# Issuing the values products of a head in one row of nine units, with eighteen probability buffers

## The reference

```
N_HEADS = 6
B, T, C = x.shape                      # 32, 1024, 96
hs = C // H                            # 16
k = (x @ Wk).reshape(B, H, T, hs)      # a plain reshape: 192 "heads" of 1024 rows
q = (x @ Wq).reshape(B, H, T, hs)
v = (x @ Wv).reshape(B, H, T, hs)
wei = einsum('bhtd,bhsd->bhts', q, k) * C ** (-0.5)
wei = where(tril(ones(T, T)), wei, -inf)
wei = softmax(wei, axis=-1)
out = einsum('bhts,bhsd->bhtd', wei, v)
```

## Time and profile before

| | before |
|---|---|
| time, median of 3 runs | 3497.25 us (3497.21 to 3500.66) |
| the profiled execution's own time | 3498.39 us |
| its span | 3496.7 us |
| TensorE busy | 3229.6 us, 92% |
| weight loads busy | 1775.0 us, 51% |
| VectorE busy | 2397.6 us, 69% |
| ScalarE busy | 2069.6 us, 59% |
| GpSimd busy | 766.1 us, 22% |
| granted TensorE clock, mean | 0.968 |

### The profile page before, as it was taken

How to read it: one execution, slowest core, us unless ns; L and a number is a source line. 1 busy time by engine, 2 the same in 40 slices (tenths; PEclk the granted TensorE clock), 3 DMA queues, 4 the chain that set the end, 5 groups by cost and what they waited for, 6 DMA issues and landing times. The chain is left out here.

```text
span 3496.7 us, 85276 instructions
## 1 busy us (share of the span) xinstructions
PE 3229.6 (92%) x28894; PEld 1775.0 (51%) x28894; DVE 2397.6 (69%) x4745; ACT 2069.6 (59%) x3730; POOL 766.1 (22%) x1529
## 2 busy tenths in 40 slices
PE   4999999999985999999999999999999989988896
PEld 2444545445542555555555555555555544443442
DVE  4566566566654777777777777777777755656665
ACT  2677777777753555555555555555555546555554
POOL 0233444444444122121221212212122100000000
PEclk8999999999997999999999999999999989989998
DMA  1122222222224555545455455554555531211221
GB/s 28 37 77 95 94 78 81 94 94 94 95 77 126 99 92 93 97 89 97 93 93 97 89 97 93 93 97 89 97 93 93 97 67 45 82 45 39 78 72 45
DMA packets 889092, 291.02 MB, mean 83 GB/s; under 512 B 840625, under 2 KB 873682, under 8 KB 889042
## 3 DMA queue, kind: packets, MB, share of 16 engines
q1 hardware_dynamic: 889042, 290.37, 37.5%
HBM read 101.55 MB, written 88.08 MB: 54 GB/s over the span
## 5 line engine op out<-in xcount | busy, mean ns | idle before, releaser
L906 ACT ACTIVATE at_probs<-at_ps_keys 128x512 f32<-128x512 f32 x1728 | 992.8, 600 | 738.7 <-PE at_ps_keys L838 616.4
L924 DVE TENSOR_REDUCE at_unit_max<-at_ps_queries 128x1 f32<-128x512 f32 (+3 forms) x2304 | 1153.7, 551 | 196.0 <-PE at_ps_queries L824 164.3
L824 PE MATMUL at_ps_queries<-at_turned 96*128 96x512 bf16 (+3 forms) x2304 | 681.5, 332 | 61.2 <-DMA at_turned<-at_spread 31.1
L838 PE MATMUL at_ps_keys<-at_turned 128*128 128x128 bf16 (+3 forms) x3456 | 660.5, 273 | 2.1 <-ACT at_probs L906 1.4
L857 PE MATMUL at_ps_values<-at_probs,at_v 128*32 128x128 f32 x13824 | 497.1, 277 | 0.1
L857 PEld LDWEIGHTS at_ps_values<-at_probs,at_v 128*32 128x32 f32 x13824 | 342.2, 109 | 134.8 <-ACT at_probs L906 68.6
L784 POOL TENSOR_TENSOR at_v<-at_stacks,at_one 128x128 f32<-128x128 f32 x192 | 77.0, 401 | 1383.6 <-PE at_ps_values L857 1341.7
L838 PEld LDWEIGHTS at_ps_keys<-at_turned 128*128 128x128 bf16 x3456 | 255.5, 97 | 223.9 <-issue 80.2
L824 PEld LDWEIGHTS at_ps_queries<-at_turned 96*128 96x128 bf16 x2304 | 191.7, 97 | 315.1 <-DVE at_unit_max L924 224.9
L827 PE MATMUL at_ps_queries<-mask_queries,ident_bf 128*128 128x128 bf16 x1536 | 330.3, 221 | 0.0
L650 PE MATMUL cb_ps_qkv<-w_attn,cb_x 96*128 96x384 f32 x512 | 198.2, 512 | 5.8 <-ACT cb_a_squares L568 4.3
(11 more groups left out here) (201 smaller groups left out, 4656.4 us busy)
## 6 DMA issues: line engine op xcount, KB each, us to landing
qkv_rows<-cb_packed SPq DMA_DIRECT2D x32, 1536.0 KB, 8.1
at_stacks<-qkv_rows SPq DMA_DIRECT2D x192, 256.0 KB, 3.3
cb_x<-in_x_dram SPq DMA_DIRECT2D x32, 384.0 KB, 3.7
cb_x_again<-in_x_dram SPq DMA_DIRECT2D x32, 384.0 KB, 4.4
x_after_conv<-cb_x SPq DMA_DIRECT2D x32, 384.0 KB, 5.0
attention_rows<-at_att SPq DMA_DIRECT2D x384, 32.0 KB, 2.2
ff_att_rows<-attention_rows SPq DMA_DIRECT2D x32, 384.0 KB, 4.0
ff_x<-x_after_conv SPq DMA_DIRECT2D x32, 384.0 KB, 4.7
```

Of the source, the lines that this page charges most:

```text
L824: mm = pe.matmul(pq[:, u % QBANKS, 0:n], QT[0:STACK, slot, qb * P:(qb + 1) * P], KT[0:STACK, slot, k0:k0 + n], start=True, stop=True)
L838: mm = pe.matmul(pk[:, bank_k, c0:c0 + n * P], KT[:, slot, kb * P:(kb + 1) * P], QT[:, slot, q0 * P:(q0 + n) * P], start=(c0 == 0), stop=True,
L906: act.activation(PR[:, slot_unit % RING, :], pk[:, slot_unit % KBANKS, :], ACT.Exp, scale=scale).then_inc(S["probs"], 1)
L924: dve.tensor_reduce(MX[:, r % 2, qb, k0 // BANK:k0 // BANK + 1], pq[:, u % QBANKS, 0:n], AX.X, ALU.max).then_inc(S["unit_max"], 1)
```

## The change

Two constants of `causal_attention` change:

```diff
     SLOTS = 4
-    RING = 6
-    BATCH_UNITS = 3
+    RING = 18
+    BATCH_UNITS = 9
     QBANKS, KBANKS = 3, 2
     LAG = 4
     VALUES_LAG = LAG + 2
```

## The result

The changed kernel takes 3576.9 us (median of 4 runs, 3574.36 to 3577.99) against 3497.23 us (4 runs): a ratio of 1.0226, 95% interval 1.0208 to 1.0244. It is 80 us slower where 59 was forecast. The profiled execution took 3576.5 us with a span of 3574.8 us, 78.1 us above the span of before.

A forecast was written before the change was run, and what follows sets the result against it. A loop over VectorE (q8 to q4) and TensorE (q7 to q8) bounds the kernel at 8.96 us a head; +1.31 - 0.40 - 0.43 - 0.17, 0.30 with exact quotients, over 190 heads plus 2 us gives 3556 us, range 3530 to 3600.

The forecast's parts named there:

- The long row: At step 5, 48 more values records between q7 and q8 add 1.31 us a head (1.18 to 1.36) to VectorE's wait.
- the rival of the slow long row: The 72 records at step 5 run slower than a short batch: +0.36 us a head, 3624 us; chance 7%.
- a batch of 72 records longer than 2.1 us: Sign at step 5 that would show the prediction wrong.
- The two turns: L813 at step 8 and L806 at step 2 come earlier; VectorE's waits of 0.40 and 0.43 us a head go.
- The rival of a late turn: L806 or L813 does not come forward, its wait stays: 0.5 us a head, 3653 us, or 3594 us; chance 8%.
- the thinner margin: At step 2, L806's output is ready some 0.2 us before VectorE's last reduction ahead of copy L937 ends.
- The regained overlap: VectorE's instructions overlap again by 0.085 us at each joint where a wait goes: 0.17 us a head, bounds 0 and 0.17.
- my own case: The forecast slowdown to 3556 us, +1.7%, with a range of its own of 3540 to 3575 us; chance 76%.
- The sum: +1.31 - 0.40 - 0.43 - 0.17, or 0.30 us a head with exact quotients, over 190 heads: +57 us, plus 2 us at the block's end.
- The loop's own share: VectorE's 0.34 us between L949 and q0, once in four heads, makes the mean head 9.09 instead of 8.96 us; left unchanged.
- The ring: Eighteen probability buffers keep nine units for step 5; ScalarE's wait on values is never late, so it costs nothing.
- Changes of shape: Two batches fewer save TensorE 0.32 us, less the turns' entries, at steps 8 and 2 where it waits: nothing gained.

The follow-up runs named there:

- the halves of the change at step 5 and step 2: Kernel before, ring of eighteen: units 3 to 8 in one row at step 5, 3548.8 us; units 0 to 5 at step 2, 3530.3 us.
- the fast order: Kernel before with L813 ahead of units 0 to 2 and units 3 to 5 right behind L806; with ring of six 3416.9 us, ratio 0.9777.
- the faster orders: Kernel before, ring of eighteen, L813 ahead of units 0 to 2; units 3 to 5 behind K8, 3467.9 us, or right behind L806, 3441.0 us.
- the second order: Kernel before, ring of eighteen, L813 ahead of units 0 to 2, units 3 to 5 right behind L806: 3441.0 us, ratio 0.9834.

## Why the prediction was right, and where it was off

**What bounds the kernel** was read rightly: the loop over VectorE from q8 to q4 and over TensorE from q7 to q8. The two runs with shortened reductions show both its extent and its edge.

**The long row** was worked out at 1.31 us more a head, all of it in VectorE's wait for q8. It measured 1.31 in the wait, 0.86 to 2.17 us, and 1.30 from q7 to q8, 1.51 to 2.81. The 72 records run at the pace of 24; the rival of the slow long row is out. The sign "a batch of 72 records longer than 2.1 us" was badly put: from the first record to q8 it is 2.10 us, but the row's records last 2.17, which is the forecast 0.86 + 1.31 itself.

**The two turns** came in time, both waits vanished, and the halves of the change at step 5 and step 2 show each alone. The rival of a late turn is out, and two products more in the thinner margin did not move the copy.

**The regained overlap** is the term of the sum that was mis-sized. The time lies in the stated range, but 2 us above the 3540 to 3575 of my own case, and the loss is 80 us, not 59. I took 0.17 us a head, 0.085 at each of the two joints, with the remark that the joints are of the same kind. The one before L941 is. The one before L937 is not: instead of 0.085 us of overlap there is a gap of 0.03. So 0.115 us a head were not regained, 22 us in all: 0.30 + 0.115 = 0.415 us, and the mean head rose by just that (9.105 to 9.520). No errors cancel here: each of the other terms is found at its size. The trace of before had the hint in it: on the copy's other side, L937 ends at 2013.72 and the next reduction starts at 2013.74, without overlap.

**The sum** then is 190 heads of 0.415 us, 79 us. The first head is 1.0 us shorter and the end of the block 1.1 us longer (it was taken at 2), so the block loses 79 us; the span grew by 78.1 and the median by 79.7, what lies before and behind the block differing by -1.7 and +0.9 us. The loop's own share stayed as it was: of four heads two take 8.97 us, one 9.10 and one 9.38, and in the changed kernel 9.38, 9.51 and 9.80. The prediction read the loop's share too simply: 0.34 us once in four heads, with the lost overlap 0.42, makes 0.10 us a head, and not the 0.13 between 8.96 and 9.09; the rest is the second head, which no row of the prediction shows. Nothing in the sum hangs on it.

**The ring** was costed at nothing. In the changed order the sum closes without it (1.31 - 0.43 - 0.40 - 0.085 + 0.03 is 0.42), but no run has the long row with a smaller ring. It does not hold elsewhere: 0.04 us a head in the order of before, 0.14 us in the fast order. ScalarE's later start is shown, and that it goes with the register instruction in front of it; that this instruction makes it late is argued.

**Changes of shape** were read at 0.10 us going in and 0.12 coming out (the row of 72 starts 0.31 us after K1's last product where the next product in the same shape follows after 0.22), and gave nothing back here because TensorE was held at those places. The forecast of the faster orders shows the limit of the account: with VectorE's waits gone, the pace passes elsewhere, most likely to TensorE and ScalarE together, and I had put it 0.2 to 0.35 us a head too low (half of it, in the second order, the ring). By how much each of them holds the other in that order stays open.

## What to carry to other kernels

When one engine feeds another through a few banks, what a long uninterrupted row costs is read from what stands behind it in the queue: add its length to the wait of the consumer there, and subtract only the waits that it used to cause elsewhere. So before lengthening rows to save changes of shape, try to put the short product that the other engine waits for ahead of each row, and next to work of its own array shape; here the two together, with the ring of six, gave 77 us, where joining the rows lost 80. A buffer that is larger than the order needs is not free by itself and is worth timing alone.

## What was not expected of the hardware

The records of VectorE's instructions overlap by 0.08 us when one follows another without a wait, but the copy of 32 partitions by 1024 that starts at partition 96 (L937) has a gap of 0.03 us on both sides, even with its input ready 0.28 us before. Enlarging the ring of ScalarE's output from 6 to 18 buffers moved some of its starts by 0.08 us, though no list of waits shows ScalarE waiting for the values products, and cost 0.14 us a head in the fast order.
